# Attention and FFN block: first Hadamard product with the matrix as weights, exponentials head by head, and new instruction orders

## The reference, cut to what matters

```python
# attention half
y   = einsum('bct,bcd->bdt', x, w1[idx1]) + bias[idx1][:, :, None]   # a 64 x 64 matrix per batch
q, k, v = y @ Wq.T, y @ Wk.T, y @ Wv.T                               # 16 heads of 32
p   = softmax(q k / sqrt(32) + alibi)                                # causal, 64 x 64 per head
x   = x + (p v) @ Wo.T
# feed-forward half
g   = einsum('bct,bcd->bdt', x, w2[idx2])
h   = hbitlinear(g, w_up)       # 512 -> 1024
h   = square(relu(h))
x   = x + hbitlinear(h, w_down) # 1024 -> 512

def hbitlinear(a, w):
    a = fwht(a)                                    # normalized Hadamard transform of the features
    s = 127 / clip(max|a| per token, 1e-5)
    a = clip(round(a * s), -127, 127) / s          # per-token quantization
    return a @ weight_quant(w).T                   # ternary weights
```

## Time and profile before

| | |
|---|---|
| time, median of 3 runs | 763.8 us |
| profiled execution: its time / its span | 763.7 us / 761.9 us |
| PE busy | 727.9 us, 96% of the span |
| DVE busy | 668.4 us, 88% |
| ACT busy | 421.9 us, 55% |
| POOL busy | 214.3 us, 28% |
| mean granted TensorE clock | 0.98 of full speed |
| length of steps 4 to 27, scores to scores | 21.54 to 21.61 us |

### The profile page before, as it was taken

One profiled execution on the slowest core, in us unless ns is written; L12 is line 12 of the kernel. 1 busy time (PEld: TensorE's weight loads), 2 busy tenths in 40 slices (PEclk: granted clock), 3 DMA queues, 4 the chain that ended last, 5 costly groups with the idle time before them and its releaser, 6 DMA issues.

```text
span 761.9 us, 23166 instructions
## 1 busy us (share of the span) xinstructions
PE 727.9 (96%) x9637; PEld 616.3 (81%) x9671; DVE 668.4 (88%) x1346; ACT 421.9 (55%) x844; POOL 214.3 (28%) x228
## 2 busy tenths in 40 slices
PE   7888999999999999999999999999999999997777
PEld 4777888888888888888888888888888888886643
DVE  3596999999999999999999999999999999988866
ACT  2478566556565565556565565565665665564421
POOL 1123333222333333222333332223333332122300
PEclk9899999999999999999999999999999999998979
DMA  7651111011111111111111110111111010110000
GB/s 235 226 182 37 37 50 41 28 34 52 49 51 50 51 49 27 40 36 51 50 50 51 51 45 23 35 49 50 50 51 50 31 31 31 30 31 16 6 11 28
DMA packets 37422, 39.91 MB, mean 52 GB/s; under 512 B 21189, under 2 KB 21317, under 8 KB 37317
## 3 DMA queue, kind: packets, MB, share of 16 engines
q1 hardware_dynamic: 34180, 32.04, 13.7%
q10 hardware_dynamic: 3136, 6.39, 2.4%
HBM read 30.02 MB, written 8.39 MB: 50 GB/s over the span
## 4 chain that ended last, share of the span: by engine, by line
PE 83%; DVE 8%; ACT 3%; POOL 2%; DMA 2%; issue 1%; SPq 1%; ACTq 0%; DVEq 0%
PE bank L367 43%; PE bank L499 8%; PE bank L535 7%; PE bank L391 4%; PE bank L357 4%; PE bank L481 4%; PE bank L508 4%; PE bank L437 4%; PE bank L454 3%; POOL gT L264 2%; DMA v_kd<-in_L_attn_Wv_dram 2%; PE bank L489 1%; DVE hid L264 1%; PE bank L519 1%; DVE hid L982 1%
## 5 line engine op out<-in xcount | busy, mean ns | idle before, releaser
L264 POOL TENSOR_TENSOR gT<-gT 128x256 f32<-128x256 f32 x124 | 107.2, 884 | 454.7 <-ACT gT L696 452.3
L264 DVE TENSOR_TENSOR hid<-hid 128x512 f32<-128x512 f32 x128 | 100.7, 828 | 0.0
L671 ACT ACTIVATE v_kd<-bank 64x256 f32<-64x256 f32 x128 | 48.5, 379 | 73.6 <-PE bank L367 72.5
L367 PE MATMUL bank<-h_hi,wk_hi 128*128 128x256 f32 x252 | 74.5, 296 | 5.6 <-ACT kT L660 5.6
L367 PE MATMUL bank<-h_hi,wq_hi 128*128 128x256 f32 x256 | 75.0, 293 | 0.0
L367 PE MATMUL bank<-h_lo,wq_hi 128*128 128x256 f32 x256 | 72.6, 284 | 0.0
L367 PE MATMUL bank<-h_hi,wq_lo 128*128 128x256 f32 x256 | 72.6, 283 | 0.0
L367 PE MATMUL bank<-h_hi,wk_lo 128*128 128x256 f32 x252 | 72.0, 286 | 0.0
L367 PE MATMUL bank<-h_lo,wk_hi 128*128 128x256 f32 x252 | 71.9, 285 | 0.0
L707 ACT ACTIVATE late<-bank 128x512 f32<-128x512 f32 x64 | 37.6, 588 | 60.3 <-PE bank L499 60.2
L1124 POOL TENSOR_TENSOR s<-s,srow 128x512 f32<-128x512 f32 x64 | 66.6, 1044 | 11.2 <-DVE srow L885 11.2
(11 more groups left out here) (126 smaller groups left out, 1946.9 us busy)
## 6 DMA issues: line engine op xcount, KB each, us to landing
x_in<-in_x_dram SPq DMA_DIRECT2D x32, 256.0 KB, 2.6
x_res<-in_x_dram SPq DMA_DIRECT2D x32, 256.0 KB, 3.4
out_dram<-late SPq DMA_DIRECT2D x32, 256.0 KB, 3.4
w_in<-in_L_cond_weights_dram SPq DMA_DIRECT2D x126, 16.0 KB, 2.4
bias_in<-in_fside_8xS_dram SPq DMA_DIRECT2D x62, 32.0 KB, 3.2
k_bd<-in_L_attn_Wk_dram ACTq DMA_DIRECT2D x1, 1024.0 KB, 5.4
s<-in_L_attn_Wq_dram ACTq DMA_DIRECT2D x1, 1024.0 KB, 6.7
v_kd<-in_L_attn_Wv_dram ACTq DMA_DIRECT2D x1, 1024.0 KB, 11.9
```

Of the source, the lines that this page charges most:

```text
L264: eng.tensor_tensor(dv[:, :, n], sv[:, :, 0], sv[:, :, 1], op).then_inc(done, 1)
L367: mm = pe.matmul(dst, lhs(a, k), rhs(b, k), start=(k == 0 and n == 0), stop=(k == KC - 1 and n == 2))
L671: ins = act.activation(v_kd[b * T:b * T + T, c % 4, e], blocks[e * T:e * T + T, :, b, :], ACT.Copy)
```

## The change

In words, part by part:
- `hadamard1` has the Hadamard matrix as weights and `g` as the moving operand. `g` is split into two f32r parts: `split_g` on ACT makes the high one, `split_g_lo` on POOL the low one. The result has features on partitions, so `q1` needn't be turned: `turn_q1` and `copy_q1t` are gone. The per-token maximum now lies across partitions. ACT copies the product (`copy_y`), DVE takes the maximum over the four blocks (`col_max1`), PE turns it (`turn_max1`), DVE reduces it, PE spreads the scale over the partitions (`spread_scale1`), and DVE applies it, rounds and clips (`apply_scale1`, `round1`, `clip1`).
- The softmax: `add_alibi` and `row_max` give the negative scores and their minimum, and `exp` is one ACT instruction per head (64 columns) with the maximum as its bias and the sum as its accumulator output. `less_max` and `exp_sum` on DVE are gone.
- The orders on PE, ACT, DVE and POOL are new; `clip2` is moved ahead of the step's end.

```diff
             def exp(c, half):
-                hs = slice(8 * half, 8 * half + 8)
-                act.wait_ge(d_less, 2 * c + half + 1)
-                act.activation(s[:, c % 2, hs, :], s[:, c % 2, hs, :], ACT.Exp).then_inc(a_exp, 1)
+                act.wait_ge(d_max, 2 * c + half + 1)
+                for j in range(8 * half, 8 * half + 8):
+                    ins = act.activation(s[:, c % 2, j, :], s[:, c % 2, j, :], ACT.Exp, bias=srow[:, 0, j:j + 1], scale=-1.0,
+                                         accum_out=srow[:, 1, j:j + 1])
+                ins.then_inc(a_exp, 1)
...
             def hadamard1(f):
-                if f == NPAIR - 1:
-                    pe.wait_ge(d_g, 4)
-                else:
-                    pe.wait_ge(p_g, 4 * f + 4)
-                for m in range(KC):
-                    mm = pe.matmul(bank[6][:, m * P:(m + 1) * P], gT[:, m, :], had, start=True, stop=True)
+                pe.wait_ge(a_ghi, f + 1)
+                pe.wait_ge(p_glo, f + 1)
+                for part in (g_hi, g_lo):
+                    mm = pe.matmul(bank[6], had_r[:, :], part[:].rearrange("p a b -> p (a b)"),
+                                   start=part is g_hi, stop=part is g_lo)
                 mm.then_inc(s_f1, 1)
-            def turn_q1(f):
...
+            def turn_max1(f):
+                pe.wait_ge(d_colmax1, f + 1)
+                pe.transpose(ps_max1, y_max[:, :], ident).then_inc(s_maxt1, 1)
+            def spread_scale1(f):
+                pe.wait_ge(d_scale1, f + 1)
+                pe.matmul(ps_scale1, sc1[:, f % 2, 3:4].broadcast_to([P, P]), ident, start=True, stop=True).then_inc(s_scale1, 1)
...
+            def split_g(f):
...
+                if f >= 1:
+                    act.wait_ge(s_f1, f)
+                act.activation(g_hi[:], gT[:], ACT.Copy).then_inc(a_ghi, 1)
+            def copy_y(f):
+                act.wait_ge(s_f1, f + 1)
+                act.activation(gT[:].rearrange("p a b -> p (a b)"), bank[6], ACT.Copy).then_inc(a_y, 1)
...
+            def split_g_lo(f):
+                pool.wait_ge(a_ghi, f + 1)
+                pool.tensor_tensor(g_lo[:], gT[:], g_hi[:].bitcast(F32), ALU.subtract).then_inc(p_glo, 1)
```

More of the change, by code:

```diff
@@ L778, in _ @@
                     copy_odd(c - 2, 0)
+                if c == 0:
+                    act.wait_ge(s_wlo, 3)
+                    copy_v(0)
+                if c == 1:
+                    copy_next_qk(1, 0)
+                if pair(c - 1):
+                    copy_g(c - 1)
+                if pair(c - 2):
                     copy_odd(c - 2, 1)
-                if next_group(c):
+                if next_group(c) and c != 1:
                     copy_next_qk(c, 0)
@@ L786, in _ @@
                 if pair(c - 1):
-                    copy_g(c - 1)
-                if pair(c):
-                    if c == 0:
-                        act.wait_ge(s_wlo, 3)
+                    split_g(c - 1)
+                if pair(c) and c > 0:
                     copy_v(c)
+                if pair(c - 1):
+                    copy_y(c - 1)
                 if next_group(c):
@@ L1042, in _ @@
                 if pair(c - 2):
-                    square_lo(c - 2, 1)
-                if pair(c):
-                    exp_sum(c, 0)
+                    back1(c - 2)
                 if pair(c - 1):
                     add_x(c - 1)
+                if pair(c):
+                    exp_recip(c, 0)
+                if pair(c) and c >= 3:
+                    row_max(c, 1)
                 if pair(c - 2):
@@ L1057, in _ @@
                     butterflies(dve, gT2[:], gT[:], 1, d_g)
+                if pair(c + AHEAD) and c > 0:
+                    dve.wait_ge(p_hlo, c + 3)
+                    add_bias(c + AHEAD)
                 if pair(c - 2):
@@ L1061, in _ @@
                     fly2(c - 2)
-                if pair(c + AHEAD) and c > 0:
-                    dve.wait_ge(p_hlo, c + 3)
-                    add_bias(c + AHEAD)
                 if pair(c):
-                    exp_sum(c, 1)
+                    exp_recip(c, 1)
                 if pair(c - 2):
                     col_max(c - 2)
-                if pair(c):
-                    exp_recip(c, 1)
                 if c == 0:
@@ L1077, in _ @@
                 if pair(c - 1):
-                    max1(c - 1)
+                    col_max1(c - 1)
                 if pair(c - 2):
```

170 lines of the change are left out of this document (87 added, 83 removed).

## The result

Changed kernel: 807.26 us median (805.71 to 807.96, 4 runs); the kernel before, measured beside it, 764.29 us (762.46 to 766.59, 4 runs). Ratio 1.0576, 95% interval 1.0545 to 1.0607: 5.8% slower. Predicted were 768.9 us (0.7% slower) and a range of 760 to 785. The sign was right; the size, 43 us in place of 5, was far off.

A forecast was written before the change was run, and what follows sets the result against it. PE, busy for 589.79 of 592 us, was taken to bound the steady steps. 763.7 + 10.0 (start) - 1.9 (steady part) - 3.0 (drain) = 768.8, as a median 768.9 us; range of 8 in 10, 760 to 785.

The forecast's parts named there:

- What bounds the kernel: Steps 3 on: PE has no hole, so its own starts set the 21.54 us step; freeing DVE alone gains nothing.
- PE in a steady step: PE's products and changes of shape: -0.08 us per step, -0.45 each in steps 28 and 29; steady part -1.9 us.
- Rival 3: PE's changes of shape cost nothing and other waits stay hidden: -0.55 in 27 steps, 753.6 us; chance 0.10.
- The exponentials: ScalarE's exponentials by head: 0.33 us per head, 2.65 for 8, in place of 0.5; low 0.24, high 0.53.
- Rival 1: ACT late in every step: at 0.44 us per head PE waits 0.5 in 27 steps, 785 us; chance 0.20.
- Does this reach PE in a steady step: Chain from cond2 to hadamard1: margin 0.35 us, nothing waits at 0.33 per head; DVE's 1.3 us loss is hidden.
- Rival 2: POOL and DVE get in each other's way: a wait of 0.35 us per step, +9.5, 778 us; chance 0.12.
- The start: Steps 0 and 1: later exponentials and new orders cost +5.1 and +4.9 us, +10.0 in all, not given back.
- Rival 4: The start catches up, as step 1 waited for the down weights' load anyway: 760.8 us; chance 0.08.
- The drain: cond2(31) to up(31) from 13.26 to 11.3 us, steps 30 and 31 about -0.5 each; together -3.0 us.

The follow-up runs named there:

- kernel 9: Changed kernel with add_bias on VectorE behind fly2 again, as before the change, in place of ahead of fly1; 784.85 us, ratio 1.0284.
- kernel 1: Changed kernel with split_g_lo on GpSimd as a one-input copy of g, the subtraction left out; 785.78 us, ratio 1.0307.
- kernel 8: Changed kernel with next_cond1 directly ahead of cond2 from step 2 on and g_lo made by a one-input GpSimd copy; 778.80 us, ratio 1.0213.
- kernel 5: Kernel before with only the exponentials changed, head by head on ScalarE, without less_max and exp_sum, old orders; 803.74 us, ratio 1.0543.
- Kernel 3: Changed kernel with add_bias(4), clip_low and the output weights' split ahead of the reciprocals on VectorE in step 0; 805.62 us, ratio 1.0560.
- kernel 10: Changed kernel with add_bias behind fly2, without keep_clock(6), and the exponentials of steps 0 and 1 as before; 777.88 us, ratio 1.0206.
- kernel 12: As kernel 10, but copy_v(0) behind step 0's second exponential and cond2(0) ahead of v_product(1); 773.85 us, ratio 1.0132.
- kernel 4: Changed kernel without the six filler products keep_clock(6) of step 32, between turn_max and turn_max1; 805.6 us, ratio 1.0551.
- kernel 2: Changed kernel with next_cond1 directly ahead of cond2 again from step 2 on; 799.31 us, ratio 1.0479.

## Why the prediction was wrong

**What bounds the kernel: right for before, and the source of the error.** "A steady step has no hole on PE" was true, and from it I took that whatever VectorE does is hidden. PE's cover was complete only while VectorE's order stayed as it was, and it had no margin even then. This is `col_max` of the same step of before:

```profile
365.07 1.99 DVE L957 TENSOR_REDUCE hid_max<-hid 128x128 f32<-128x1024 f32 x1
```

It ends at 367.06, and its reader `turn_max` starts on PE at 367.12, 0.06 later, and so in each of the steps 4 to 27. In the changed kernel, where PE does wait for it, the distance is the same 0.06.

**PE in a steady step: right to about 0.1.** Predicted -0.08. Without its 0.95 of waits the changed step is 21.58 against 21.54, and kernel 9 has 21.62 and more. Steps without `next_cond1` were to gain 0.45. In kernels 1 and 8 steps 28 and 29 took 20.95 against 21.49, but in before 0.26 of the 21.49 are a wait at `hadamard1`, so PE's own work fell by about 0.3. In the changed kernel these two steps gained nothing (21.61): PE waits 0.59 at `hadamard1` for g_lo. *Rival 3*, changes of shape cost nothing, is out: `cond2` alone takes 0.62 to the next start, and no steady step was under 21.6.

**The exponentials: right,** 0.33 per head. *Rival 1*, ACT late in every step, didn't happen in the changed order: `hadamard1` has no wait. It did happen in kernel 5, where the order was not changed: so the new order of `copy_g` is what hides them.

**Does this reach PE in a steady step: the step that failed,** -1.9 us predicted for steps 3 to 29, +25.6 measured, and 1.1 more in step 2. I followed one chain, `cond2` to `hadamard1`, to 0.1 us, and summed VectorE up in a sentence ("It loses about 1.3 us per step, which PE's 99.6% hide"). The work that it loses was about right (1.4), the hiding was not. `turn_max1` is a new instruction on PE that waits for VectorE, so VectorE's chain had to be followed up to it: `next_cond1`, `add_bias`, `fly1`, `fly2`, `col_max`, `col_max1`. *Rival 2* (GpSimd and VectorE get in each other's way, 778) had the mechanism, but looked for it at `hadamard1`, where the changed kernel has it only in steps 28 and 29, priced it at 0.35 per step, and had a chance of 0.12. The trace of before already had the price: in the earlier trace rows `turn_g` is 3.44 for four, where the same four in the start take 2.94, and in the same step of before `fly2` is 1.82 while `fly1`, ahead of `turn_g`, is 1.29. These are rows of the kernel before, DVE:

```profile
360.79 1.29 DVE L264 TENSOR_TENSOR hid<-hid 128x512 f32<-128x512 f32 x2
...
362.13 1.82 DVE L264 TENSOR_TENSOR hid<-hid 128x512 f32<-128x512 f32 x2
```

**The start: near in sum, partly by luck,** +10.0 predicted, +11.3 measured. The second reciprocal of step 0 came at 49.15 (48.5), `pv(1)` at 80.54 (78.9). But the parts are 0.6 ahead of scores(0), 6.9 in step 0 and 3.7 in step 1, where 5.1 and 4.9 were predicted. And the wait named for step 0, `turn_p(0, 0)` for the late `add_bias(4)`, is only 1.01 us; the larger one, 4.01, is PE's wait for the copy of k, which stands on ScalarE behind the exponentials and `copy_v`. Kernel 3, which moved `add_bias` forward, gained nothing clear; kernels 10 and 12, which put back ScalarE's exponentials and places, gained. What was not priced is the clock: after the wait of 4.01 us PE runs at 0.51 of full speed. In another execution with the same step 0 (kernel 9) the clock was back at 1.00 in the window 50 to 54, and step 0 took 19.16 in place of 21.00. So up to 1.8 us of step 0 differ from one execution to the next, and the clock with them; at scores(2) 0.9 of that was left. *Rival 4*, the start catches up, is out: scores(2) kept all of it, and step 3 lost 0.8 beyond the 0.99 of every step.

**The drain: wrong in sign,** -3.0 predicted from step 30 on, +5.4 measured: 1.0 in step 30 and 4.4 behind scores(31), of which 3.1 lie between `cond2(31)` and `up(31)` (16.39 against 13.26). PE, DVE and, in the third fence, POOL of the kernel after; the last fence is DVE of before:

```profile
772.99 0.47 PE L486 MATMUL bank<-g_hi,had_r 128*128 128x512 f32 x1 [2.97 <-POOL g_lo L1178]
...
775.96 0.48 PE L524 MATMUL bank<-cst_sb,hid_max 128*128 128x128 f32 x1 [2.26 <-DVE hid_max L990]
776.23 2.77 PE L384 MATMUL bank<-up_w 128*128 128x512 bf16 x6
778.79 0.42 PE L492 MATMUL bank<-cst_sb,y_max 128*128 128x128 f32 x1
```
```profile
771.76 2.23 DVE L269 TENSOR_TENSOR hid<-hid 128x512 f32<-128x512 f32 x2
774.03 1.87 DVE L990 TENSOR_REDUCE hid_max<-hid 128x128 f32<-128x1024 f32 x1
```
```profile
771.26 1.58 POOL L1178 TENSOR_TENSOR g_lo<-gT,g_hi 128x512 fp32r<-128x512 f32 x1 [19.03 <-ACT g_hi L725]
```

```profile
730.80 1.87 DVE L957 TENSOR_REDUCE hid_max<-hid 128x128 f32<-128x1024 f32 x1
```

`col_max` ends 9.27 after the start of `cond2(31)` (766.63), where it took 7.39 before: `fly2` takes 2.23 beside g_lo in place of 1.29, and VectorE starts the butterflies of g 0.94 later behind `cond2`. Then the six filler products, 0.46 each at a granted clock of 0.50, stand ahead of `turn_max1`, worth 1.5 us (4). The new links themselves are not the cause: without the filler, from the end of `col_max` to `up(31)` is 5.60 in kernel 4 and was 5.87 before. My estimate had held neither the wait between GpSimd and VectorE nor the filler.

**What stays open.** The span of kernel 12 is 9.6 us above before's: 1.65 in the start, 1.0 in step 3, 3.5 in the steady steps, 1.0 in step 30 and 2.4 behind scores(31). Their causes were not tried one by one. Nor was an order in which `turn_g` falls on no VectorE instruction with two inputs in SBUF.

## What to carry to other kernels

A busy bounding engine hides another engine's work only as long as nothing on it starts to wait for that engine: for each new instruction with a wait, follow the whole chain behind the wait, on every engine that it crosses, also where the engine at its end gets less to do. When work moves between GpSimd and VectorE, lay their instructions with two operands in SBUF side by side in time: here they run one after the other. And where an instruction waits for another engine, put it as late in its queue as its reader allows: `add_bias`, moved behind `fly1`, `fold1` and `fly2`, was worth 22 us.

## What the runs showed of the hardware

- A VectorE subtraction or addition of 128x512 with both inputs in SBUF takes 0.68 us alone. Beside a GpSimd instruction that started before it, it ends 0.54 to 0.56 after that one ends. Of the instructions of `fly1` and `fly2` in the fourteen traces, all 858 that started so keep to this, and the other 934 take 0.68 to 0.69: 1.78 beside a two-input subtraction of 1.40, 1.10 beside a copy of 0.73. So a one-input instruction of GpSimd holds it up too, for as long as it runs. GpSimd waits likewise, and an addition of 128x256 that starts beside a running `fly1` or `fly2` ends about 0.6 after it: `turn_g` takes 2.94 in the changed kernel, where one of its four meets `fly1`, 3.92 where all of `fly1` falls on it (kernel 2).
- An exponential of 64 columns with pointer bias and accumulator is followed after 0.33 us, its 0.19 read included.
- TensorE's granted clock fell from full speed (2.4 GHz) to its lower level (1.2 GHz), 0.51 and 0.52 in the windows shown, beside waits of 4.01 and 3.92 us in steps 0 and 1. Before the change (longest wait 1.40 us), and in kernel 12 (1.84 us), it stayed at 1.00 in the same steps. In kernels 5 and 10 it also fell, with longest waits of 2.81 and 2.19 us.
